# Halves dumped earlier, and the first tile's transposes moved one step forward, in an xDeepFM kernel

## The reference

```python
emb = tables[feat_idx, sparse]                       # 2048 x 26 x 32
linear_out = lin_sparse_w[feat_idx, sparse].sum(-1) + dense @ lin_dense_w
x0 = emb; xk = emb
for w, bb in ((conv1_w, conv1_b), (conv2_w, conv2_b)):
    hp = einsum('bhd,bmd->bhmd', xk, x0).reshape(-1, h * M, E)
    xn = sigmoid(einsum('oi,bid->bod', w, hp) + bb[None, :, None])
    half = xn.shape[1] // 2                          # 64 of 128
    xk = xn[:, :half]; res.append(xn[:, half:])
cin_out = (concatenate(res, 1).sum(-1) @ cin_w + cin_b)[:, 0]
deep_x = concatenate([emb.reshape(-1, M * E), dense], -1)
h1 = tanh(deep_x @ W1 + b1); h2 = tanh(h1 @ W2 + b2); h3 = tanh(h2 @ W3 + b3)
return linear_out + cin_out + (h3 @ deep_w + deep_b)[:, 0] + bias[0]
```

## Time and profile before

| | before |
|---|---|
| median of 3 runs | 1602.87 us |
| profiled execution, its time | 1607.53 us |
| profiled execution, span | 1605.7 us |
| mean granted clock of TensorE | 0.993 |
| TensorE matmul busy | 1515.2 us (94%) |
| VectorE busy | 1133.7 us (71%) |
| ACT busy | 646.7 us (40%) |
| POOL busy | 682.6 us (43%) |
| bytes moved by DMA | 322.08 MB, 201 GB/s |

### The profile page before, as it was taken

The page is one execution under the profiler, slowest core; times in us unless marked ns, Lnnn a source line. Parts: engine busy times, 40 slices in busy tenths (PEclk is TensorE's granted clock), DMA queues, the critical chain, the costliest instruction groups (busy, mean ns, idle before and its releaser), DMA issues.

```text
span 1605.7 us, 23632 instructions
## 1 busy us (share of the span) xinstructions
PE 1515.2 (94%) x6552; PEld 662.5 (41%) x6552; DVE 1133.7 (71%) x1113; ACT 646.7 (40%) x904; POOL 682.6 (43%) x600
## 2 busy tenths in 40 slices
PE   0598999999999999999999999999999999999999
PEld 0233333333333333333333333333333337787876
DVE  3385878788888887878787877788876785343442
ACT  2333443444444344334444443434443433444443
POOL 7356564546464646454555546464631010000000
PEclk9998999999999999999999999999999999999999
DMA  6686989888998899988898989898999993846741
GB/s 130 132 228 170 230 217 222 197 232 204 241 216 233 201 232 198 233 200 232 206 241 208 236 198 236 203 247 200 246 194 240 234 243 105 187 129 167 166 134 53
DMA packets 177869, 322.08 MB, mean 201 GB/s; under 512 B 30160, under 2 KB 106032, under 8 KB 177796
## 3 DMA queue, kind: packets, MB, share of 16 engines
q1 hardware_dynamic: 128250, 287.98, 70.8%
q10 hardware_dynamic: 36273, 26.61, 6.9%
q0 software_dynamic: 13312, 7.06, 4.4%
HBM read 300.24 MB, written 21.31 MB: 200 GB/s over the span
## 4 chain that ended last, share of the span: by engine, by line
PE 75%; DMA 9%; issue 4%; DVE 3%; SPq 2%; ACTq 2%; POOL 2%; ACT 1%; another core or an unknown queue 0%; DVEq 0%; POOLq 0%
PE acc L800 37%; PE acc L794 16%; PE bc L937 14%; DMA x0t<-x_halves 6%; PE bc L780 4%; PE bc L787 3%; ACTq L388 2%; POOL emb L572 2%; DMA emb<-table,idx_stage 2%; SPq L490 1%; DVE xb L747 1%; DVE hp L747 1%; DMA x_halves<-deep_halves 1%; PE bc L772 1%; DMA xb<-x_rows 1%
## 5 line engine op out<-in xcount | busy, mean ns | idle before, releaser
L572 POOL DMA_INDIRECT emb<-table,idx_stage x416 | 494.8, 1189 | 335.9 <-DVE hp L747 169.9
L747 DVE TENSOR_TENSOR hp<-bc,xk 128x1024 f32<-128x1024 f32 x384 | 446.3, 1217 | 257.1 <-PE bc L780 172.7
L747 DVE TENSOR_TENSOR xb<-xb,xk 128x1024 f32<-128x1024 f32 x448 | 552.4, 1288 | 15.1 <-DMA xb<-x_rows 14.9
L800 PE MATMUL acc<-xb,w2s 128*64 128x512 f32 x1792 | 408.6, 594 | 0.2
L800 PE MATMUL acc<-hp,w2s 128*64 128x512 f32 x1536 | 362.9, 608 | 6.0 <-ACT r L986 6.0
L794 PE MATMUL acc<-sq,w1s 128*128 128x512 f32 x768 | 349.9, 605 | 2.2 <-issue 2.2
L979 ACT ACTIVATE sq<-bc 128x1024 f32<-128x1024 f32 x192 | 182.9, 1027 | 190.2 <-PE bc L787 144.0
L800 PEld LDWEIGHTS acc<-xb,w2s 128*64 128x64 f32 x1792 | 127.1, 137 | 253.3 <-issue 227.0
L583 POOL TENSOR_TENSOR r<-r 128x512 f32<-128x512 f32 x96 | 128.8, 1342 | 220.6 <-ACT r L990 130.3
L794 PEld LDWEIGHTS acc<-sq,w1s 128*128 128x128 f32 x768 | 141.9, 191 | 181.3 <-issue 181.3
L984 ACT ACTIVATE xk<-acc,bias 64x512 f32<-64x512 f32 x128 | 87.3, 682 | 275.9 <-PE acc L794 164.1
(11 more groups left out here) (61 smaller groups left out, 814.0 us busy)
## 6 DMA issues: line engine op xcount, KB each, us to landing
xb<-x_rows SPq DMA_DIRECT2D x448, 256.0 KB
xb<-x_rows SPq DMA_DIRECT2D x192, 512.0 KB
w_raw<-W SPq DMA_DIRECT2D x48, 512.0 KB
xb<-x_rows SPq DMA_DIRECT2D x128, 128.0 KB
x0t<-x_halves ACTq DMA_DIRECT2D x252, 52.0 KB
x_full<-x_halves SPq DMA_DIRECT2D x96, 128.0 KB
x_halves<-deep_halves ACTq DMA_DIRECT2D x30, 384.0 KB
emb<-table,idx_stage POOLq DMA_INDIRECT x416
```

The source lines that it names most:

```text
L572: nc.gpsimd.indirect_dma_start(out=emb[:, m, :], out_offset=None, in_=table, in_offset=bass.IndirectOffsetOnAxis(ap=idx_stage[:, m:m + 1], ...
L747: nc.vector.tensor_tensor(product(n)[:, :], x[:, :], xk[sl % 2][:, :], ALU.mult).then_inc(multiplied, 1)
L800: last = nc.tensor.matmul(acc_y[H * c:H * c + H, :], w2s[:, ORDER[n], :], src[:, c * CHUNK:(c + 1) * CHUNK], start=(n == 0), stop=(n == PA ...
```

## The change

It does four things. The deep step is now the second step of tile 0 too, with an order of its own (`FIRST_TILE_WORK`): the transposes stand between the two groups of the squares, the products 2 to 4 of the step behind fills 5 to 7, and VectorE makes the lower halves before product 5. In tile 0 the halves are dumped by SP in the third step, behind the first group of copies; in the other tiles ACT dumps them in the second step directly behind `read_y2`, where it did so in front of `read_xn` of the second group. `load_next_rows` of the third step stands in front of `read_y2`, as it does in the steps before. And the gathers are spread differently: in tile 0 six more are tied to signals of the first squares, and in the tiles after it the last one begins with the 13th product of the step before the next tile.

```diff
--- before.py
+++ after.py
+FIRST_TILE_WORK = (
+    ("fill", (("K", 0), ("K", 1), ("K", 2))),
+    ("of_last", (5, 6, 7)),
+    ("of_last", (8, 9, 10, 11, 12)),
+    ("fill", (0, 1, 2)),
+    ("first", 0),
+    ("fill", (("D", 0), ("D", 1), ("D", 2))),
+    ("first", 1),
+    ("of_this", (0, 1)),
+    ("fill", (5, 6, 7)),
+    ("of_this", (2, 3, 4)),
+)
+DEEP_STEP = 1
...
@@ -101,19 +115,17 @@
-def deep_step(ahead):
-
-    return 2 if ahead == 3 else 1
+def step_work(sl, ahead):
+
+    if ahead == 0 and sl == STEPS - 1:
+        return FINAL_WORK
+    return FIRST_TILE_WORK if ahead == 3 and sl == DEEP_STEP else STEP_WORK
 
 
 def step_fills(sl, ahead):
 
-    fills = [use for kind, what in STEP_WORK if kind == "fill" for use in what]
-    if ahead == 0 and sl == STEPS - 1:
-        fills = [use for use in fills if not is_k(use)]
-    if ahead == 0 or sl != deep_step(ahead):
-        fills = [use for use in fills if not is_d(use)]
-    return fills
+    fills = [use for kind, what in step_work(sl, ahead) if kind == "fill" for use in what]
+    return fills if ahead > 0 and sl == DEEP_STEP else [use for use in fills if not is_d(use)]
...
@@ -388,6 +400,14 @@
+        def dump_halves(eng, t):
+            for i in range(2):
+                eng.dma_start(x0_halves[bass.ds(t, 1), i, 0:(KD - 1) * P, :].rearrange("t (k p) b -> p (t k) b", p=P),
+                              deep_halves[:, i, 0:KD - 1, :].bitcast(F32)).then_inc(halves_dumped, 16)
+            eng.dma_start(x0_halves[bass.ds(t, 1), :, (KD - 1) * P:M * ROW, :].rearrange("t i p b -> p (t i) b"),
+                          deep_halves[0:LAST_E, :, KD - 1, :].bitcast(F32)).then_inc(halves_dumped, 16)
...
@@ -508,7 +528,11 @@
                             sp.wait_ge(contracted, contracted_by(s - 1, ns[-1]))
                             hold()
                         spread_by_dma(t, sl, i)
-                    if sl == deep_step(ahead) and ahead > 0:
+                        if is_first and sl == DEEP_STEP + 1 and i == 0:
+                            sp.wait_ge(deep_lowered, 2 * DEEP_N)
+                            hold()
+                            dump_halves(sp, t + 1)
+                    if sl == DEEP_STEP and ahead > 0:
                         dump(t + 1)
 
                     if ahead == 1:
@@ -612,24 +636,26 @@
                 if is_first:
                     free_emb(t, DEEP_N)
                     gather(range(8), gathered)
-                    gather_in(s, range(8, 16), range(8))
+
+                    for m, (signal, count) in enumerate(((k_contracted, 1), (xk_made, 1), (xk_made, 2), (squared, K1 + 1),
+                                                         (squared, K1 + 2), (squared, 2 * K1))):
+                        pool.wait_ge(signal, count)
+                        hold()
+                        gather((8 + m,), gathered)
+                    gather_in(s, range(14, M), (0, 1, 2, 3, 4, 4, 4, 4, 5, 6, 7, 8))
                     add_up(t, 1, r1, r1_step, xn_read, 2, sum1)
-                    gather_in(s, range(16, 21), range(8, PAIRS))
-                    gather_in(s + 1, range(21, M), range(5))
                     add_up(t, 2, r1, r1_step, xn_read, 2, sum1)
+                    free_emb(t + 1, filled_by(t, DEEP_STEP, ("D", DEEP_N - 1), ahead))
                     add_up(t, 1, r2, r2_step, y2_read, 1, sum2)
-                    free_emb(t + 1, filled_by(t, 2, ("D", DEEP_N - 1), ahead))
                     gather_in(s + 2, range(5), (1, 2, 3, 4, 6))
                     add_up(t, 3, r1, r1_step, xn_read, 2, sum1)
                     gather_in(s + 2, range(5, 11), range(7, PAIRS))
                     add_up(t, 2, r2, r2_step, y2_read, 1, sum2)
-                    gather_in(s + 3, range(11, 20), range(9))
+                    gather_in(s + 3, range(11, 22), (0, 1, 1, 2, 3, 3, 4, 5, 6, 7, 7))
                     return
                 if ahead > 0:
-                    gather_in(s - 1, range(20, 23), (8, 10, 12))
+                    gather_in(s - 1, range(22, M), (8, 9, 10, 12))
                 add_up(t - 1, STEPS - 1, r2, r2_step, y2_read, 1, sum2)
-                if ahead > 0:
-                    gather_in(s, range(23, M), (0, 1, 3))
                 add_up(t, 1, r1, r1_step, xn_read, 2, sum1)
                 if ahead > 1:
                     free_emb(t + 1, filled_by(t, 1, ("D", DEEP_N - 1), ahead))
@@ -639,13 +665,13 @@
                     gather_in(s + 1, range(4, 8), (7, 8, 10, 12))
                 add_up(t, 1, r2, r2_step, y2_read, 1, sum2)
                 if ahead > 1:
-                    gather_in(s + 2, range(8, 11), (0, 2, 4))
+                    gather_in(s + 2, range(8, 12), (0, 2, 4, 6))
                 add_up(t, 3, r1, r1_step, xn_read, 2, sum1)
                 if ahead > 1:
-                    gather_in(s + 2, range(11, 15), (7, 8, 10, 12))
+                    gather_in(s + 2, range(12, 17), (7, 8, 9, 10, 12))
                 add_up(t, 2, r2, r2_step, y2_read, 1, sum2)
                 if ahead > 1:
-                    gather_in(s + 3, range(15, 20), (0, 2, 4, 6, 7))
+                    gather_in(s + 3, range(17, 22), (0, 2, 4, 6, 7))
 
...
@@ -726,7 +752,7 @@
                     for n in range(PAIRS):
-                        if n == 0 and sl == deep_step(ahead) and ahead > 0:
+                        if n == (5 if is_first else 0) and sl == DEEP_STEP and ahead > 0:
                             dve.wait_ge(gathered, t * GATHERED + GATHERED)
                             sum_linear(t + 1)
                             for i, ks in enumerate(DEEP_PARTS):
...
@@ -865,7 +891,7 @@
                     there = step_fills(sl, ahead)
-                    for kind, what in FINAL_WORK if final else STEP_WORK:
+                    for kind, what in step_work(sl, ahead):
                         if kind == "fill":
...
@@ -1020,10 +1036,6 @@
                     there = step_fills(sl, ahead)
-                    turning = sl == deep_step(ahead) and ahead > 0
-
-                    late = turning and sl == 2
-
                     def load_next_rows():
                         if sl < 2 or ahead > 0:
...
@@ -1033,8 +1045,8 @@
                             for c in range(2):
                                 load_rows(act, t + (sl + 2) // STEPS, (sl + 2) % STEPS, c)
 
-                    for kind, what in STEP_WORK:
-                        if kind == "of_last" and what[-1] == PAIRS - 1 and ("K", 0) in there and sl != 2:
+                    for kind, what in step_work(sl, ahead):
+                        if kind == "of_last" and what[-1] == PAIRS - 1 and ("K", 0) in there:
                             load_next_rows()
                         if kind == "fill":
...
@@ -1057,17 +1069,12 @@
                                 act.wait_ge(r2_step, t * SUMS - (SUMS - 1))
                             if sl == STEPS - 1 and not is_first:
                                 act.wait_ge(r2_step, t * SUMS - (SUMS - (STEPS - 1)))
-                            if late:
-                                dump_halves(t + 1)
                             read_y2(s - 1, (sl - 1) % STEPS)
-
-                            if sl == 2 and not late:
-                                load_next_rows()
+                            if sl == DEEP_STEP and ahead > 0 and not is_first:
+                                act.wait_ge(deep_lowered, t * DEEP_N + 2 * DEEP_N)
+                                act.sem_inc(act_held, 1)
+                                dump_halves(act, t + 1)
                         elif kind == "first" and ("K", 0) in there:
-                            if turning and not late and what == 1:
-                                dump_halves(t + 1)
-                            if late and what == 1:
-                                load_next_rows()
                             act.wait_ge(k_contracted, k_contracted_by(s, what))
                             if what == 0:
```

More of the change, by code:

```diff
@@ L990, in read_y2 @@
                 nc.scalar.activation(r2[:, sl, :], acc[sl % 2][:, :], ACT.Sigmoid, bias=bias2[:, :]).then_inc(y2_read, 1)
-            def dump_halves(t):
-                act.wait_ge(deep_lowered, t * DEEP_N + DEEP_N)
-                act.sem_inc(act_held, 1)
-                for i in range(2):
-                    act.dma_start(x0_halves[bass.ds(t, 1), i, 0:(KD - 1) * P, :].rearrange("t (k p) b -> p (t k) b", p=P),
-                                 deep_halves[:, i, 0:KD - 1, :].bitcast(F32)).then_inc(halves_dumped, 16)
-                act.dma_start(x0_halves[bass.ds(t, 1), :, (KD - 1) * P:M * ROW, :].rearrange("t i p b -> p (t i) b"),
-                             deep_halves[0:LAST_E, :, KD - 1, :].bitcast(F32)).then_inc(halves_dumped, 16)
             act.wait_ge(ident_loaded, IDENT_LOADED)
```

## The result

| | before | changed |
|---|---|---|
| median, runs | 1604.05 us, 4 | 1665.58 us, 4 |
| lowest to highest | 1598.68 to 1613.62 | 1654.72 to 1667.13 |
| profiled execution: time, span | 1607.53, 1605.7 | 1664.67, 1662.9 |
| mean granted clock of TensorE | 0.993 | 0.978 |

The ratio is 1.0362, 95% interval 1.0296 to 1.0429. The prediction (1589, range to 1612) was wrong, and the case that it had named as the slower rival came, a little beyond its heavy end (1651).

What follows compares the result with a forecast made beforehand. TensorE was taken as the bound in the tile loop, so only its idle time could be won: -26.7 + 3.8 + 6.9 + 2 = -14.0 us against the profiled 1607.53, carried to the median as 1589 us. Range 1575 to 1612.

Steps and rivals of the forecast that it cites:

- the slower rival: Tiles 1 to 14: dump issues hold ACT before the first group's read; named with 1623 us, 1651 at heaviest; chance 0.13.
- Other tiles, the dump moved ahead of the reads of the squares' sums: Second steps: third dump issue delays read_xn(0), 0.3 us in 11 tiles and 1.2 in 3; 6.9 us lost.
- The case written for 7.6 us of hold: Slower rival's heavy end: every tile 3.5 us late plus 1.4 for the clock, 69 us instead of 6.9, 1651 us.
- the other terms: Later tiles: waits won for x0t 6.8, L986 6.0, gathers 2.2, and clock 1.3; 2 us kept for late dumps.
- the decisive point: Slower rival: from 5.4 us between first dump issue and third's return, 14 tiles cost 18 us.
- Tile 0: First tile, transposes moved to its second step: 10.4 us won, 3.8 lost to a new wait and the clock.
- The 1.4 for the clock: Tile 0's third step: slower clock after the new 2.4 us wait for the bank read, costing 1.4 us.
- Loads ahead of the bank read: Third steps: earlier row loads end 6.8 us of x0t waits and 6.0 for L986; 2 us kept in two tiles.
- the second rival: Halves land late in the third step as a rule, 14 tiles waiting 1.2 us each: 1604 us; chance 0.17.
- Gathers: Gathers kept out of the next tile's first product: 2.2 us of transposes' waits go, at no cost.
- The packet rule: DMA engines serve queues packet by packet, so the dump skips SP's backlog: 6.9 us becomes 0, time 1582.

Runs made afterwards that it cites:

- short copies: Changed kernel with SP's copies in the second step of tiles 1 to 14 cut to 24 of 128 partitions, output not the reference's: 1584.52 us profiled, one run.
- the loads away: Changed kernel with the second step's four row loads issued on SP's queue ahead of its copies, tiles 1 to 14: 1620.99 us, 1.0062 of the kernel before.
- third issue later: Changed kernel with only the 90 KB dump issue put in front of the second group's read_xn, tiles 1 to 14: 1597.52 us, 0.9924 of the kernel before.
- 90 KB first: Changed kernel with the 90 KB dump issue ahead of the two of 384 KB: 1598.25 us, 0.9943 of the kernel before.
- dump back: Changed kernel with the dump in front of the second group's read_xn again, tiles 1 to 14: 1615.62 us, 1.0041 of the kernel before.
- the dump and the loads both back: Changed kernel with dump and third-step row loads in their old places, tiles 1 to 14: 1605.99 us, 1.0002 of the kernel before.

## Why the prediction was wrong

- **The step that failed** is "Other tiles, the dump moved ahead of the reads of the squares' sums": the cost of the hold on ACT, put at 6.9 us in all; it was 74.4. The working there gave 0.7 us late for a third issue of 3.60 and 3.5 for 6.31. The median became 6.03. I scaled it down, because "the third issue returns after the copies issued before the dump have drained", and at the new place fewer of SP's nine copies had been issued. At the old place the packets fit that reading: of the two queues only SP's moved anything until the issue returned, in 14 of 15 dumps. What failed is the scaling: a shorter line in front did not make a shorter hold. At the old place SP had issued its last copy when the dump was issued (968.1 against 968.58), at the new one it was in the middle of them (923.39 in 920.70 to 926.95), and its packets went on beside the dump's. With short copies the same issue takes 0.85 us, with the loads away 4.42. How much of the growth from 3.60 to 6.03 belongs to the copies issued later isn't measured by itself.
- **Its price**: the 14 waits behind the dump are 53.0 us, and the hp matmuls were busy 21.4 longer in a slower clock, 3.8 and 1.5 a place. The case written for 7.6 us of hold had 3.5 and 1.4, 14 x 4.9 = 69 us and 1651: the right prices for what came. The middle lost 64.1 where the other terms should have won 14.3 (6.8 + 6.0 + 2.2 + 1.3 - 2), so 78.4 in place of 69.
- **Its weight**: the rival had 0.13 and the decisive point, 5.4 us between first issue and return, which is a third issue of 4.2. The row of before had 3.60 in the median and 6.31 at the most: with such a spread the point lay inside the row, and 0.13 was too little, the more so as no row showed the queue at the new place. Its reason, the x0t loads of the same queue, was a part (hold 4.42 without them).
- **Tile 0** was right: 10.4 won and 3.8 back gave 6.6, measured 148.89 - 142.29 = 6.6. The dump was taken to land near 109.7 from 102.4, 7.3 us; ACT's loads behind it start at 111.39, 8.0 after 103.35. The wait for read_y2 was 1.75 (2.4 taken). The 1.4 for the clock did not come at that wait (6 matmuls took 2.84 us on either side of it), so that the sum fits to a tenth is in part luck.
- **Loads ahead of the bank read** was right for the 6.8 us of x0t waits, which went, and came back when the loads were put back. Its price, 2 us in two tiles, was not: in the changed kernel no wait for read_y2 came after tile 0, but in the runs without the hold in front of the first read it did, 12.9 us in 3 waits (third issue later), 8.3 in 2 (90 KB first), 14.5 in 5 (dump back). They are in third steps, and with the dump and the loads both back 0.3 us of them is left. This is the second rival, the halves that land late, in some tiles. With the 90 KB first, ACT stood in front of the loads of tile 9's third step until the halves had landed at 825.1, 24 us after their first issue at 801.05 (15.5 taken), and the squares waited 6.53 us, to 829.66. Two rows, of the chain that ended last and of ACT's timeline:

```profile
802.24 22.84 DMA x_halves<-deep_halves
...
825.25 3.55 ACTq L400 DMA_DIRECT2D x0t<-x_halves  x4
```

- **Gathers**: 2.2 us of waits became 0.9. Right in kind, too small to see in time; with the dump back and with the third issue later one wait of 4.0 us for a gather came.
- **The total without the hold** would have been -20.9 by my sum (1.3%). Measured with the 90 KB first it is 0.57% (0.26 to 0.88), under half of it. That kernel still waits 8.3 us for read_y2 in place of 2, and 4.5 us for the first reads in place of 0. Why the halves land so late in some tiles only is open.
- **The packet rule** of the Trainium skill (DMA: Bandwidth & Descriptors, Queues, rings and completion order), by which the queues take turns packet by packet, was weighed only for the wait behind SP's backlog, where it gave 0 of hold. The trace agrees with the turns once the dump's pieces run (136 packets to 135 in 929 to 931), but not with a hold of 0: the first piece came 4.09 us after the issue, and the turns with SP's copies made the rest slow while ACT stood.

Open is what exactly is full, and what ends the hold. 948 pieces ahead did not hold the last issue in any tile (1.76 us at most), 1280 did in the median (3.75), but with as little as 0.65; and behind 1536 with the loads on SP's queue two of 14 took 0.98 and 1.00. So no single number of pieces decides it, and the runs don't name the cause.

## What to carry to other kernels

A DMA issue isn't free on the engine that makes it: here, behind two transfers of 384 KB in pieces of 512 B, it stood there for 3.84 to 11.03 us. So move such a dump only with its issue durations (median and maximum) in hand, and ask which instruction stands behind the last issue at the new place, and what other queues move at that time. Put the small transfer first, which here took the hold away, or the last one where nobody waits behind it. When a row's spread spans the point that decides, give that rival weight by the spread, not by the median.

## What was unexpected of the hardware

- The order of three issues of the same bytes changed the time by 4%: 384, 384, 90 KB held ACT 6.03 us in the median, 90, 384, 384 KB at most 1.76 us, 384, 90, 384 KB at most 0.98.
- The length of the hold followed what stood ahead (6.03, 3.75, 0.72 us behind 768, 640 and 384 KB) and what ran beside it (0.85 us behind 768 KB with short copies). At the old place it ended before a single piece of the dump had started.
- 3.54 us of idle time of TensorE was followed by 5.17 us at a granted clock of 0.50: this stall cost 1.7 times its length. Over the 14 places it was 1.4 times.
- Once they met, ACT's dump and SP's copies went in turn, 136 packets of SP's to 135 of ACT's in 2 us, though SP's carried 0.44 MB and ACT's 0.07.
